# A chain of sparse products on one core: 16 gather slots, a written-out gather loop, and VectorE's masks ahead of the running sums

## What is computed

```python
def prop(z):
    return jax.ops.segment_sum(edge_weight[:, None] * z[src], dst, num_segments=N_SUP)
for i in range(5):                      # layers
    z = h @ W[i] + b[i]
    x_start = prop(z)
    xi = h
    for _ in range(5):                  # rounds
        xi = (prop(xi) + x_start) / 2.9
    mean = jnp.mean(xi, axis=0)
    var = jnp.var(xi, axis=0)
    out = gamma[i] * (xi - mean) / jnp.sqrt(var + 1e-5) + beta[i]
    h = jnp.where(out > 0, out, 0.01 * out)
```

## Time and profile before

| | |
|---|---|
| median of 3 runs | 11559.22 us (11555.72 to 11560.43) |
| span of the profiled execution | 11598.4 us |
| PE busy | 7734.7 us, 67% |
| DVE busy | 6797.1 us, 59% |
| POOL busy | 7123.4 us, 61% |
| ACT busy | 1197.8 us, 10% |
| granted TensorE clock, mean | 0.659 of full |

### The profile page before, as it was taken

One profiled execution on the slowest core, in us unless ns is written; L12 is line 12 of the kernel. 1 busy time (PEld: TensorE's weight loads), 2 busy tenths in 40 slices (PEclk: granted clock), 3 DMA queues, 4 the chain that ended last, 5 costly groups with the idle time before them and its releaser, 6 DMA issues. The chain is left out here.

```text
span 11598.4 us, 175759 instructions
## 1 busy us (share of the span) xinstructions
PE 7734.7 (67%) x38121; PEld 5090.7 (44%) x38121; DVE 6797.1 (59%) x24532; ACT 1197.8 (10%) x2596; POOL 7123.4 (61%) x7294
## 2 busy tenths in 40 slices
PE   4633377788777797777877778877779177660090
PEld 2423233357333475333663345743337055560070
DVE  5644655567555576555665556765556666450176
ACT  0122000001000011000010000100000511440005
POOL 5756366663666664666636666456666466766664
PEclk8755555679555697555785556965559578785555
DMA  3133354432444424444334444244543522662106
GB/s 126 44 126 142 91 91 92 92 70 69 92 92 92 90 49 95 91 92 92 61 76 93 92 92 81 58 95 92 91 93 52 178 62 63 174 174 36 24 28 268
DMA packets 1057829, 1076.56 MB, mean 93 GB/s; under 512 B 193805, under 2 KB 913982, under 8 KB 1057648
## 3 DMA queue, kind: packets, MB, share of 16 engines
q0 software_dynamic: 211200, 395.39, 22.0%
q1 hardware_dynamic: 723504, 525.23, 14.3%
q10 hardware_dynamic: 123072, 155.41, 4.3%
HBM read 565.26 MB, written 522.63 MB: 94 GB/s over the span
## 5 line engine op out<-in xcount | busy, mean ns | idle before, releaser
L864 POOL DMA_INDIRECT G<-tab,ridx x5000 | 4746.3, 949 | 3013.2 <-issue 2328.4
L981 PE MATMUL PS<-G,lring 128*1 128x128 f32 x10000 | 2411.0, 361 | 1504.0 <-DMA G<-tab,ridx 1470.1
L356 DVE SCALAR_TENSOR_TENSOR G<-G,whole,PS 1x128 f32<-1x128 f32 (+1 forms) x4050 | 1353.8, 334 | 2568.5 <-PE PS L981 1977.4
L995 PE MATMUL PS<-G,M 128*128 128x128 f32 x10000 | 2780.8, 418 | 45.5 <-DVE G L356 44.0
L995 PEld LDWEIGHTS PS<-G,M 128*128 128x128 f32 x10000 | 2155.6, 274 | 684.6 <-issue 376.4
L981 PEld LDWEIGHTS PS<-G,lring 128*1 128x1 f32 x10000 | 556.1, 85 | 3071.0 <-DMA G<-tab,ridx 2721.0
L377 DVE TENSOR_SCALAR M<-keyrow,keycol,wccol 128x128 f32 (+1 forms) x5004 | 1393.6, 350 | 1.0
L956 ACT COPY big<-PS 128x512 f32 x250 | 146.4, 585 | 7147.2 <-PE PS L991 7147.2
L688 ACT ACTIVATE big<-big,nb,rs 128x128 f32<-128x128 f32 x1564 | 614.8, 479 | 935.4 <-POOL nb L679 911.8
L948 DVE TENSOR_TENSOR Y<-PS,big 128x512 f32<-128x512 f32 x1000 | 679.4, 679 | 0.0
L356 DVE SCALAR_TENSOR_TENSOR carry<-G,whole,PS 1x128 f32<-1x128 f32 (+1 forms) x1350 | 451.2, 334 | 182.0 <-DVE G L356 0.3
(11 more groups left out here) (387 smaller groups left out, 9973.5 us busy)
## 6 DMA issues: line engine op xcount, KB each, us to landing
tab<-Y SPq DMA_DIRECT2D x1250, 256.0 KB, 3.1
G<-tab,ridx POOLq DMA_INDIRECT x5000, 3.3
big<-agg SPq DMA_DIRECT2D x90, 832.0 KB, 6.4
x<-big ACTq DMA_DIRECT2D x60, 832.0 KB, 3.6
big<-x SPq DMA_DIRECT2D x60, 832.0 KB, 4.8
xt_d<-big ACTq DMA_DIRECT2D x30, 858.0 KB, 7.7
x2n<-big ACTq DMA_DIRECT2D x30, 838.5 KB, 3.5
big<-x2n SPq DMA_DIRECT2D x30, 838.5 KB, 5.3
```

What stands on the lines that cost most here:

```text
L356: nc.vector.scalar_tensor_tensor(carried if jj == GR else row0(j), row0(j - 1), whole[0:1, bass.ds(tile + jj - 1, 1)], local(jj - 1), ALU. ...
L864: pool.indirect_dma_start(G[:, j, 0:D], None, tab_in(k), bass.IndirectOffsetOnAxis(ap=ridx[:, j:j + 1], axis=0)).then_inc(l_got[j], 16)
L981: nc.tensor.matmul(PS[0:1, CAR, j % GR, :], lring[:, j:j + 1], G[:, j, 0:D], start=True, stop=True).then_inc(l_row, 1)
L995: ins = nc.tensor.matmul(PS[:, SUM + h, j % GR, :], M[:, j, :], G[:, j, 0:D], start=True, stop=True)
```

## The change

`G` gets RG = 16 slots in place of 8. The gather loop of a round is written out (200 gathers in a row), reads the column of `gidx` itself (no `ridx`, no `l_idx`), and waits once in eight gathers: from tile 16 on, ahead of every even group, for the sums (`l_sum`) and the carry (`l_ch`) of the group three before it. The programs of DVE and PE run in bodies of four groups (NG), LI = 12 passes and two more groups written out; their slots follow q, their masks, `lring`, `Y` and the SUM banks still h. DVE builds the masks of the next group ahead of the running sums, no longer between them and the eviction. The credit is gone.

```diff
+RG = 16
+NG = RG // GR
+LI = T // RG
+LREM = (T - LI * RG) // GR
-        G = sb("G", [P, U, D + HEADS])
+        G = sb("G", [P, RG, D + HEADS])
 ...
-        l_got = pool_sems("l_got", U)
+        l_got = pool_sems("l_got", RG)
 ...
         def l1_gather(pool, l, k):
-            r0 = rounds(l, k)
+            g0 = 2 * rounds(l, k)
             steady(pool, 16 * rounds(l, k + 1))
             for h in range(2):
                 pool.wait_ge(l_tab[h], 16 * rounds(l, k + 1))
-            with pool.Fori(0, IT) as i:
-                for j in range(U):
-                    g = 2 * (r0 + i) + j // GR
-                    steady(pool, g + 1)
-                    if j % GR == 0:
-                        pool.wait_ge(l_idx, g + 1)
-                        pool.wait_ge(l_sum, g + 1)
-                    pool.indirect_dma_start(G[:, j, 0:D], None, tab_in(k), bass.IndirectOffsetOnAxis(
-                        ap=ridx[:, j:j + 1], axis=0)).then_inc(l_got[j], 16)
+            for t in range(T):
+                if t >= RG and t % U == 0:
+                    free = g0 + (t - RG) // GR + 2
+                    steady(pool, free, OPS * free + 1)
+                    pool.wait_ge(l_sum, free)
+                    pool.wait_ge(l_ch, OPS * free + 1)
+                pool.indirect_dma_start(G[:, t % RG, 0:D], None, tab_in(k), bass.IndirectOffsetOnAxis(
+                    ap=gidx[:, t:t + 1], axis=0)).then_inc(l_got[t % RG], 16)
 ...
+        def group_loop(eng):
+            with eng.Fori(0, LI) as i:
+                for q in range(NG):
+                    yield i, q
+            for q in range(LREM):
+                yield LI, q
+
+        def got_before(l, k, slot):
+            return (LI + (1 if slot < GR * LREM else 0)) * (NL * l + k)
 ...
         def l1_dve(dve, l, k):
-            with dve.Fori(0, IT) as i:
-                for h in range(2):
-                    g = 2 * (r0 + i) + h
-                    running_sums(dve, g, U * i + GR * h, h, lambda j: G[0:1, j, 0:D],
-                                 lambda jj: PS[0:1, CAR, jj, :], carry[:, 0:D], l_row, l_ch)
-                    nc.vector.tensor_copy(lring[:, GR * h:GR * h + GR],
-                                          lastc[:, bass.ds(U * i + U + GR * h, GR)]).then_inc(l_lr, 1)
-                    nc.vector.tensor_copy(ridx[:, GR * h:GR * h + GR],
-                                          gidx[:, bass.ds(U * i + U + GR * h, GR)]).then_inc(l_idx, 1)
-                    for j in range(GR):
-                        ins = edge_mask(U * i + GR * (h + 1) + j, GR * (1 - h) + j, wccol)
-                    ins.then_inc(l_mask, 1)
-                    dve.wait_ge(l_sum, g + 3)
+            for i, q in group_loop(dve):
+                h, g, tile = q % 2, g0 + NG * i + q, RG * i + GR * q
+                dve.wait_ge(l_sum, g)
+                for j in range(GR):
+                    ins = edge_mask(tile + GR + j, GR * (1 - h) + j, wccol)
+                ins.then_inc(l_mask, 1)
+                running_sums(dve, g, tile, 0, lambda j, q=q: G[0:1, GR * q + j, 0:D],
+                             lambda jj: PS[0:1, CAR, jj, :], carry[:, 0:D], l_row, l_ch)
+                nc.vector.tensor_copy(lring[:, GR * h:GR * h + GR],
+                                      lastc[:, bass.ds(tile + U, GR)]).then_inc(l_lr, 1)
+                dve.wait_ge(l_sum, g + 1)
 ...
         def l1_pe(pe, l, k):
-                        pe.wait_ge(l_got[j], 16 * (r0 + i) + 16)
-                        nc.tensor.matmul(PS[0:1, CAR, j % GR, :], lring[:, j:j + 1], G[:, j, 0:D],
+                    pe.wait_ge(l_got[s], 16 * (got_before(l, k, s) + i) + 16)
+                    nc.tensor.matmul(PS[0:1, CAR, j, :], lring[:, GR * h + j:GR * h + j + 1], G[:, s, 0:D],
                                          start=True, stop=True).then_inc(l_row, 1)
 ...
-                credit(l_sum, 2)
-                nc.vector.tensor_copy(ridx[:], gidx[:, 0:U]).then_inc(l_idx, 2)
```

More of the change, by code:

```diff
@@ L54, in build @@
 def build(nc, x0, src, dst, ea, ew, w0, b0, w1, b1, gamma, beta, w2, b2, we, be, coef, linw, linb, asrc, adst, out):
-    assert T * TE == E and IT * U == T and CHUNKS * NJ == NC_ and CHUNKS % 2 == 0
+    assert T * TE == E and IT * U == T and LI * RG + LREM * GR == T and NG % 2 == 0 and LREM % 2 == 0 and CHUNKS * NJ == NC_ and CHUNKS % 2 == 0
     ctx = ExitStack()
@@ L821, in build @@
         ZB_, HZB = (PA, PA + 1), (PB, PC)
-        l_w, l_wr, l_col, l_base, l_idx, l_mask, l_lr, l_ch, l_row, l_sum, l_ev, l_xt, l_xc, l_yl, l_sq = (
-            sem("l_" + n) for n in "w wr col base idx mask lr ch row sum ev xt xc yl sq".split())
-        l_got = pool_sems("l_got", U)
+        l_w, l_wr, l_col, l_base, l_mask, l_lr, l_ch, l_row, l_sum, l_ev, l_xt, l_xc, l_yl, l_sq = (
+            sem("l_" + n) for n in "w wr col base mask lr ch row sum ev xt xc yl sq".split())
+        l_got = pool_sems("l_got", RG)
         l_tab, l_u, l_h, l_z, l_hz = (sems("l_" + n, 2) for n in "tab u h z hz".split())
@@ new lines, in l1_dve @@
+            for i, q in group_loop(dve):
[9 more added lines that the diff above has]
+                dve.wait_ge(l_sum, g + 1)
+                if last:
+                    nc.vector.tensor_copy(group_of(Y, h), PS[:, SUM + h, :, :]).then_inc(l_yl, 1)
+                    dve.wait_ge(l_yl, 2 * IT * l + NG * i + q + 1)
+                    nc.vector.tensor_tensor(SQ[h][:], group_of(Y, h), group_of(Y, h), ALU.mult).then_inc(l_sq, 1)
+                else:
+                    dve.wait_ge(l_tab[h], 16 * (rounds(l, k + 1) + NG // 2 * i + q // 2))
+                    nc.vector.tensor_tensor(group_of(Y, h), PS[:, SUM + h, :, :],
+                                            zt[:, bass.ds(tile * D, GR * D)].rearrange("p (s f) -> p s f", f=D),
+                                            ALU.add).then_inc(l_ev, 1)
@@ L967, in l1_pe @@
         def l1_pe(pe, l, k):
-            r0 = rounds(l, k)
+            g0 = 2 * rounds(l, k)
             last = k == NL - 1
[L970 to L979, removed]
-                        pe.wait_ge(l_got[j], 16 * (r0 + i) + 16)
-                        nc.tensor.matmul(PS[0:1, CAR, j % GR, :], lring[:, j:j + 1], G[:, j, 0:D],
[L982 to L994, removed]
-                        ins = nc.tensor.matmul(PS[:, SUM + h, j % GR, :], M[:, j, :], G[:, j, 0:D],
-                                               start=True, stop=True)
-                    ins.then_inc(l_sum, 1)
-                    if last:
-                        pe.wait_ge(l_sq, gl)
-                        node_sums(pe, U * i + GR * (h - 1), 1 - h)
```

36 lines of the change are left out of this document (27 added, 9 removed).

## The result

The changed kernel takes **11,010.9 us** (median of 4 runs, 11,008.2 to 11,013.6) against 11,557.5 for the kernel before, measured beside it: ratio 0.9528, interval 0.9514 to 0.9541. The prediction was 10,950 in a range from 10,900 to 11,130. The profiled execution of the changed kernel spans 11,011.7 us, 587 less than the one of before. In medians the gain is 547.

The account below looks back on a forecast made before the run. GpSimd was taken as the bound at 1.253 us a gather, plus slot waits and drains. Plain rounds 496, last rounds 111 and drains 2 make 609 us off the median 11,559.2: 10,950 us, range 10,900 to 11,130.

Parts of the forecast that it names:

- The bound and the wait: GpSimd's gathers in plain rounds: 1.253 us each, 249.3 us a round; slot waits of 24.3 us a round go.
- Rival D: GpSimd's waits for slots do not go, half of the gain: about 11,250 us; chance 0.04.
- The plain round: The twenty rounds with k < 4: 260.0 us each against 284.8, a gain of 496 us in all.
- drain: Between rounds, from last gather to the next first one: 10.75 us instead of 11.25.
- The last rounds: Round k = 4 of each of five layers: 253 us against 275.3, bounds 249 and 260, gain 111 us.
- From the span to the median: The 609 us gain taken off both the profiled span (11598.4) and the median (11559.2), 39 us less.
- rival A: GpSimd's written-out gathers stall for instruction fetch: up to 200 us, about 11,130 us; chance 0.11.
- By itself the new order gains nothing: VectorE's masks ahead of running sums: DVE's cycle 4.30 us (before 3.8), PE's 4.1, both under GpSimd's 5.01.
- B, the chain becomes the bound: DVE and PE set the pace at 5.3 us a group: 360 us lost, about 11,310 us; chance 0.08.
- C, gathers slow down: Masks on DVE stretch GpSimd's gathers, one in four by 0.53 us: 660 us lost, about 11,610; chance 0.03.
- The slower side: The chance that the changed kernel is slower than before: 0.03, all from gathers slowed by VectorE's masks.

Follow-up runs that it names:

- slots8: The changed kernel with 8 slots instead of 16, each group of gathers waiting for the group two before it: 11,543.95 us, ratio 1.0025.
- old_order: The changed kernel with VectorE's masks moved back behind the running sums and lring, ahead of the eviction; 16 slots stay: 11,008.8 us, ratio 0.9561.
- order_only: The kernel before with only VectorE's masks moved ahead of the running sums, still 8 slots: 11,579.7 us, ratio 1.0056.
- loop16: The changed kernel with gathers in a loop of 16 again and indices copied by VectorE to a 16 wide ridx: 11,053.96 us, ratio 0.9599.

## Why the prediction was right, and where it was off

**The bound and the wait: right.** GpSimd's pitch is the bound: 199 steps take 249.2 to 250.0 us in the first layer's plain rounds (249.3 in the prediction). The waits for slots went with the slots and came back with slots8. Rival D is refuted by the 71.7 us, most of it pitch.

**The plain round: 260.7 instead of 260.0.** Two errors cancel in part. The drain came out at 10.3 us in the mean (10.75 predicted from one drain of 11.25; the mean before was 11.55), as the eviction no longer stands behind the masks; with VectorE's old order it is 10.9. But the pitch of 1.253 was read in one layer and isn't that of all: rounds take 251.3 us of issue in the second layer and 252.1 in the third (compare 1041.50 and 1049.60 above). Summed, the gain was 483 us instead of 496.

**The last rounds: 255.3 instead of 253**, within the bounds of 249 to 260. The gain was 100 us instead of 111; this is the mis-sized term. Over the pitch the five take 27 us more, where 4 each were guessed. 11 of the 27 are gathers stretched by VectorE's square, which the prediction put at nothing although one had taken 1.473 us before. 14 are gaps longer than 0.30 us. These fit the clock: at the start of such a round PE's products and node sums can take over 6 us a group while it is low (0.91 in the slower window above, 0.95 in the faster), and GpSimd waits. But in old_order the same gaps come to 2 us and the stretched gathers to 20, so the new order seems to have a part in them. In sum the span's gain was 587 instead of 609, 22 us off.

**From the span to the median: 39 us off, the largest error.** The prediction took the gain of one profiled execution off the median, which lay 39 us below that execution's span. After the change, span and median agree (11,011.7 and 11,010.9). An execution that is slower than the median of its kernel is slower somewhere, and if that is in the very waits that the change takes away, the difference goes with them. The sum "span before less gain" (10,989) was the better number for the median too. That the 39 us lay in those waits is likely, not shown: the kernel before varies from 11,501 to 11,560 over two chips, while the changed kernel and old_order stay within 11,002 to 11,014.

**How near it was.** The forecast missed by 61 us, and the result lies at the upper end of the forecast's own range (11,010), which stood for last rounds at 260 us and an unchanged drain; neither came. What leaves it well inside the stated range is the room up to 11,130, made for rival A, which didn't come either. (By A's own price of 200 us that end would be 11,150.)

**"By itself the new order gains nothing": right in its sum, wrong in its price.** VectorE's cycle was worked out as 4.30 us; the timeline shows 4.29 in a group where it sets the pace. It was weighed against 5.01 in the one case with 16 slots, and there the order is neutral (old_order). It was not weighed for what it takes away as cover: with 8 slots it costs 65 us (order_only), and where PE's signals come late it costs 453 us with three gathers a group.

**Rivals.** *A, code fetch:* the packets rose from 53 to 134 as foreseen, and the gaps stay at 0.307 us in the mean; loop16 fetches 83 and is not faster. *B, the chain becomes the bound:* false on the first chips but for a few groups; on the later two the kernel does wait for PE and VectorE, by a mechanism that the prediction did not have. *C, gathers slow down:* from the masks by some 0.01 us in the mean, from the squares in a few (below). *The slower side:* it was given 0.03 for C. It happened, on two chips, where PE's signals come late; how much of it is the exposed wait is open.

## What to carry to other kernels

When the bound engine has a fixed pitch, count slots by the whole way of a slot (three further issues, landing, products, signal) against the time in which they are wanted again; one step more than that freed the whole wait here. Work that stands under a wait for another engine is cover even where the wait looks short in the profile at hand: put it behind the wait only if something is gained by it. And measure such a change on more than one chip, since the one that decides may not be the one that was profiled. Last, where a trace misses signals, add up an engine's idle rows before you read one of them.

## What was not expected of the hardware

**A square on VectorE holds a gather that starts just behind it.** All 27 gathers over 1.15 us in the changed kernel lie beside VectorE's square of the last rounds, a product of a tile in SBUF with itself. They are just those that start 0.04 to 0.3 us behind the start of a square. The 212 that overlap one and start earlier than that keep their time (0.96 us at most), and the 28 that start later pay at most 0.16 us. In the changed kernel:

```profile
6750.65 0.69 DVE L934 TENSOR_TENSOR OT<-Y 128x512 f32<-128x512 f32 x1
6750.78 1.38 POOL L844 DMA_INDIRECT G<-tab,gidx  x1 [0.30 <-issue]
```

1.38 us instead of 0.95: the gather pays 0.43 of the square's 0.69. What it pays is what is left of the square at its start (0.56 here), less 0.13 us. That holds within 0.02 us for each of the 27, for the 56 in old_order and for the 79 in order_only. Over the changed kernel this is some 11 us, over order_only 36. In old_order no mask runs beside any of the 56, so it is the square and not the masks behind it. The Trainium skill (SBUF — State Buffer, "SBUF: two separate sides") names a lock by operations of VectorE with two inputs in SBUF, against a GpSimd operation that reads SBUF; a gather reads its index column there, and these traces agree that the later of the two waits, if it is the gather, and that a gather that came first is not touched. It names two-port operations as well. Whether the masks are one no run shows, but they aren't quite free: 163 of the 1766 gathers beside masks alone take 1.00 to 1.08 us, and none of the 2967 beside neither reaches 1.00.

**PE's signals can be late.** On the two later chips the eviction waits up to 4.64 us in the lines above, and four signals of PE come within 0.2 us of the one that was late. In the changed kernel's plain rounds 46% of the 1000 evictions there start over 1 us behind the products, in the first profile none. VectorE's signals are not late in those lines: PE goes on 0.35 us behind its copy to lring (4302.67 + 0.15 to 4303.17). The kernel before takes 13,114 us instead of 11,515, and its first gather of these layers starts at 1420.9 us instead of 1326.5, so the stages ahead are slower too. Whether it is the chips, or something else about these later runs, stays open; no run varied it.

**The pitch of the gathers differs by layer** with the same code: 1.252, 1.260, 1.263, 1.252 and 1.252 us in the five layers of the changed kernel. In before, old_order, slots8, order_only and loop16 each is 0.003 us less, with the same steps between layers. No experiment touched this.
